# Message layer of a graph network kernel: five sums of halves moved between radial groups, and the rotation of older sums moved behind the new rotated features

## The reference

```python
x = _layernorm(x + _L0_gnn_ref(x, src, dst))        # mean of x[src] over the edges of each node
R = relu(edge_weight[:, None] @ w1 + b1) @ w2 + b2   # 64 hidden, 384 radial weights of each edge
# per edge: features x[src] = 8 scalars and 8 vectors; messages are sums over
# R * (spherical harmonics of the edge's direction) * features, by angular momentum
out = zeros.at[dst].add(msg)
x = _layernorm(x + out)
```

## Time and profile before

| | us |
|---|---|
| median of 3 runs | 4083.58 (4083.02 to 4086.64) |
| profiled execution, its own time | 4087.7 |
| its span | 4086.0 |
| PE busy | 3442.0 (84%) |
| DVE busy | 3366.2 (82%) |
| POOL busy | 2994.6 (73%) |
| ACT busy | 694.0 (17%) |
| message layer, from the first gather to the last batch | about 1830 to 3910 |

### The profile page before, as it was taken

One profiled execution on the slowest core, in us unless ns is written; L12 is line 12 of the kernel. 1 busy time (PEld: TensorE's weight loads), 2 busy tenths in 40 slices (PEclk: granted clock), 3 DMA queues, 4 the chain that ended last, 5 costly groups with the idle time before them and its releaser, 6 DMA issues.

```text
span 4086.0 us, 47708 instructions
## 1 busy us (share of the span) xinstructions
PE 3442.0 (84%) x14069; PEld 1822.3 (45%) x14069; DVE 3366.2 (82%) x4410; ACT 694.0 (17%) x1038; POOL 2994.6 (73%) x3050
## 2 busy tenths in 40 slices
PE   1988888888988888537999999999999999999963
PEld 0544444444444444333444444444444444444443
DVE  8877777767767776657999999999999999999965
ACT  0111111111111111101222212222222222122210
POOL 2777777777777777677777777777777777777747
PEclk9999999999999999658999999999999999999975
DMA  3111111111111111111222222222222222222211
GB/s 74 39 29 39 31 39 28 39 29 40 29 29 38 31 39 28 30 35 41 52 58 58 58 57 53 55 58 58 58 56 52 58 58 58 57 53 55 58 31 24
DMA packets 169732, 185.26 MB, mean 45 GB/s; under 512 B 57906, under 2 KB 136805, under 8 KB 163175
## 3 DMA queue, kind: packets, MB, share of 16 engines
q1 hardware_dynamic: 72486, 134.98, 11.8%
q0 software_dynamic: 97216, 49.97, 8.7%
HBM read 122.11 MB, written 62.61 MB: 45 GB/s over the span
## 4 chain that ended last, share of the span: by engine, by line
POOL 30%; issue 16%; PE 6%; DVE 2%; DMA 0%; POOLq 0%; DVEq 0%; ACT 0%
POOL got L559 27%; PE ps_r L822 3%; POOL hid L535 2%; PE ps_m L796 2%; PE ps_m L813 1%; DVE prod L1393 1%; DVE unit L1342 0%; DVE prod L1385 0%; DMA got<-x_d,idx 0%; DVE x_room L1342 0%; PE ps_m L805 0%; DVE part L1363 0%; POOLq L565 0%; POOLq L554 0%; DVE runs L1176 0%
## 5 line engine op out<-in xcount | busy, mean ns | idle before, releaser
L559 POOL DMA_INDIRECT got<-x_d,idx x1568 | 1575.2, 1005 | 510.3 <-issue 496.1
L822 PE MATMUL ps_r<-wc,hid 128*128 128x384 f32 x3136 | 1114.9, 494 | 136.8 <-DVE prod L1393 123.1
L822 PEld LDWEIGHTS ps_r<-wc,hid 128*128 128x128 f32 x3136 | 580.8, 190 | 677.4 <-DVE prod L1393 252.3
L1385 DVE TENSOR_TENSOR prod<-ps_r,f_along 128x768 f32<-128x768 f32 (+1 forms) x588 | 505.1, 859 | 105.3 <-PE ps_r L822 77.3
L750 PE MATMUL ps_r<-rest_f,hid 128*128 128x448 bf16 x1372 | 512.3, 373 | 0.2
L750 PE MATMUL ps_r<-inv_len,hid 128*128 128x448 bf16 x1372 | 510.1, 372 | 0.0
L750 PE MATMUL ps_r<-w_sb,hid 128*128 128x448 bf16 x1372 | 508.3, 370 | 0.0
L1393 DVE TENSOR_TENSOR prod<-ps_r,f_across 128x768 f32<-128x768 f32 (+1 forms) x588 | 505.6, 860 | 0.0
L512 POOL DMA_INDIRECT got<-in_x_dram,idx_deep x364 | 356.7, 980 | 184.0 <-issue 104.9
L512 POOL DMA_INDIRECT f_along<-in_x_dram,idx_deep x364 | 345.4, 949 | 111.0 <-issue 104.3
L512 POOL DMA_INDIRECT f_across<-in_x_dram,idx_deep x364 | 344.3, 946 | 111.0 <-issue 103.7
(11 more groups left out here) (189 smaller groups left out, 4199.5 us busy)
## 6 DMA issues: line engine op xcount, KB each, us to landing
run_d<-runs_t SPq DMA_DIRECT2D x196, 256.0 KB
hid<-weight_t SPq DMA_DIRECT2D x98, 512.0 KB, 5.8
got<-x_d,idx POOLq DMA_INDIRECT x1568
frame_d<-x_sb SPq DMA_DIRECT2D x7, 1008.0 KB, 4.4
frame<-frame_d SPq DMA_DIRECT2D x98, 72.0 KB
frame_b<-frame_d SPq DMA_DIRECT2D x98, 72.0 KB, 1.9
got<-in_x_dram,idx_deep POOLq DMA_INDIRECT x364, 2.4
f_along<-in_x_dram,idx_deep POOLq DMA_INDIRECT x364, 2.4
```

Source lines behind the costliest of these rows:

```text
L559: pool.indirect_dma_start(got[k][:, t, :], None, x1_d, bass.IndirectOffsetOnAxis(ap=idx[k][:, t:t + 1], axis=0)).then_inc(got2_landed[k], 16)
L822: mm = pe.matmul(ps_r[:, g % 2, t, 0:RD], hid[k][:, col:col + P], wc[:, :], start=True, stop=True)
L1385: dve.tensor_tensor(prod[q][:, 0:size, 0:2, :, :], ps_r[:, q, 0:size, 0:256].rearrange("p t (b v u) -> p t b v u", b=2, u=MUL), spread(f_a ...
```

## The change

On PE the sums of halves between the groups are (3), (4, 5) and (6, 7) in place of (3, 4), (5, 6) and (7). On DVE the rotation back of batch b - 2 comes behind the new rotated features in place of ahead of them.

```diff
                     radial(b, k, 2)
                     if not isinstance(b, int) or b > 0:
-                        add_halves(b - 1, 1 - k, (3, 4))
+                        add_halves(b - 1, 1 - k, (3,))
                     radial(b, k, 3)
                     if not isinstance(b, int) or b > 0:
-                        add_halves(b - 1, 1 - k, (5, 6))
+                        add_halves(b - 1, 1 - k, (4, 5))
                     radial(b, k, 4)
                     if not isinstance(b, int) or b > 0:
-                        add_halves(b - 1, 1 - k, (7,))
+                        add_halves(b - 1, 1 - k, (6, 7))
                     radial(b, k, 5)
...
                         halve(b - 1, 1 - k, GROUPS - 1)
-                    if not first:
-                        turn_back(b - 2, k)
                     s.settle()
                     s.mark(dve.tensor_tensor(part[:, 0], part[:, 0], part[:, 1], ALU.add))
                     s.settle()
...
                     dve.tensor_tensor(f_across[k][:, :, 0, :, :], part[:, 0, :, 1:3, :], part[:, 2, :, 1:3, :],
                                       ALU.add).then_inc(rotated_in, 1)
+                    if not first:
+                        turn_back(b - 2, k)
                     dve.wait_ge(f0_copied, b + 1)
                     dve.wait_ge(rotated_in, b + 1)
```

## The result

| | us |
|---|---|
| before, median of 4 runs | 4084.61 (4083.02 to 4086.64) |
| after, median of 4 runs | 4147.04 (4135.96 to 4173.83) |
| ratio | 1.0162, 95% interval 1.0140 to 1.0184 |
| predicted | 4184, range 4072 to 4245 |
| profiled run of after | 4173.83, span 4172.1 |

The change made the kernel 1.6% slower. The profiled run of after is the slowest of its four, so its trace shows somewhat more than the median pays. First the page of after: span, busy shares, the chain that ended last, and the group of the gathers.

What follows compares the result with a forecast made beforehand. Before, GpSimd and the VectorE/TensorE loop were taken as equally long; after, GpSimd bounds: 22.2 against 21.17 us over 97 batches, +100 us, 4188 for the profiled execution, 4184 as median, range 4072 to 4245.

Steps and rivals of the forecast that it cites:

- Steps 1 to 3: Message layer: regrouped halves and later rotation back bring the DVE and PE loop from 21.04 to 20.18 us.
- A3: DVE's first product of the fourth group, forecast 12.29 us after the batch's parts begin, before 13.14.
- GpSimd becomes the bound: Message layer: without holds GpSimd needs 20.30 us a batch, already more than the 20.18 of DVE and PE.
- The holds: Time gathers are held up by VectorE instructions with both inputs in SBUF; bounds 0.94 and 2.5 us a batch.
- by any phase: Mean hold if gathers start anywhere in the batch: 0.104 us a gather, 1.66 a batch.
- walked: Gather starts followed one by one from the parts: holds 2.1 us, then 2.0; 22.3 a batch with stops.
- The prediction's condition: A gather starting while VectorE runs an instruction with both inputs in SBUF is held until about 0.12 us before its end.
- the stops: GpSimd halts for about 2 us once in 112 gathers, 0.28 us a batch.
- step 1: PE: one half instead of two between radial 2 and radial 3, taking 0.86 us off the loop.
- A: Rival: GpSimd sheds its holds, 20.30 to 20.8 us a batch, 4000 to 4048 us; chance 0.14.
- B: Rival: the phase stays lucky or radial 3 gains nothing, 21.2 to 21.4 a batch, 4086 to 4106 us; chance 0.16.
- C: Rival: each batch collides with the hid load and holds reach 2.5, 22.8 a batch, 4242 us; chance 0.10.

Runs made afterwards that it cites:

- experiment 3: After, with SyncE's 512 KB load of hid queued behind the load of frame_b, nothing left out: 4104.3 us, 1.0047 of before.
- experiment 2: VectorE's part alone: before, with only the rotation back moved behind f_across, the halves as they were: 4162.2 us, 1.0179 of before.
- experiment 5: After, with two extra products of the third group, making VectorE's loop 0.94 us longer: 4154.9 us, 1.0177 of before.
- experiment 1: TensorE's part alone: before, with only the halves regrouped as 3, 4 to 5 and 6 to 7: 4097.6 us, 1.0027 of before.
- experiment 6: After, with each sum of halves replaced by a one-input copy of the first half, the second left out: 4122.5 us, 1.0099 of before.

## Why the prediction was right, and where it wasn't

The direction, the place and GpSimd as the bound came as forecast, the size was 37 us lower, 4147 in place of 4184, for the profiled execution 14 us. The traced execution took 4173.8 where the sum gave 4188 for it; what makes the other three runs 25 to 38 us shorter than that one, no trace shows, but their granted clock over the whole run is 0.925 to 0.926 against its 0.919, which fits fewer late landings.

- **Steps 1 to 3, the loop of DVE and PE.** Forecast A3 at 12.29, period 20.18; measured 12.11 and 20.18 in an undisturbed batch. Right.
- **GpSimd becomes the bound.** Right: 44 late landings for 127 us were measured where 40 or more for over 130 were named, and experiment 3 shows each batch beginning on GpSimd's last landing.
- **The holds.** Forecast 1.66 by any phase and 2.1 walked; measured 1.46. The walk's single holds are in the traces to 0.03 us (experiment 2). Why the mean of after is lower is mostly the 104 gathers that begin with an instruction and aren't held: held, they would bring it to 2.08 by the estimate above, near the walk's 2.1. The prediction's condition ("starts while VectorE runs" such an instruction) gave them no exception. That a late landing moves GpSimd to phases that cost less (a phase is where in DVE's batch the gathers begin) shows in VectorE's part alone and in experiment 5 (1.03 and 0.97 of holds in batches that waited, 1.94 and 1.80 in the others), hardly in after (1.38 and 1.51). L559's mean of 1036 ns is below the 1045 named.
- **Further idle.** Forecast 0.28 for the stops; measured 0.63, and this is the term that was missing. A late landing can cost more than the wait: in 24 of the 44 TensorE's clock falls behind it, the fourth product waits for up to 2.9, and GpSimd, then ahead, is stopped at its third gather for the radial groups (57 us against 12). For the same reason L1385's waits for PE were not nearly gone (53 us). The two misses had opposite signs: 1.46 + 0.63 = 2.09 against a chosen 22.2 - 20.0 = 2.2. That the sum came so near is in part luck.
- **The cause as the prediction divided it.** It let the shorter loop (step 1) bring the loss and took the rotation's place for harmless in itself. That step failed: the rotation's place alone costs 1.8%, TensorE's part alone 0.3%. The prediction had named the windows that the new order puts together, but not asked what they cost at the old loop. That a shorter loop raises the holds isn't refuted by this: with the free starts counted in, the old order would pay 0.33 more of them a batch in experiment 1, and it is these free starts that kept the holds there at 0.83.
- **Rivals.** A fell (the change brought more holds, not fewer), B fell (holds of 1.46 where it kept them near 1, and a fourth product that came earlier), C was partly there: 44 of 93 batches wait for a landing, not each.
- **The condition for a hold** was too narrow on one side (experiment 6), which changed nothing in the sum, since no one-input copy runs in this layer, and too wide on the other, at an instruction's beginning, which did.

Shown by runs: that the rotation's place carries the loss (experiment 2), that the load of hid beside a last landing costs 0.40 of idle (experiment 3), and that VectorE's work doesn't set the time (experiment 5). Read from traces and not tested by itself: what the free starts save, what the fall of the clock costs apart from the landing, and what a late landing does to the phase. The table's figures of holds and idle come from one profiled execution of each kernel. The run that would have shown GpSimd as the bound directly, after with 15 gathers, ran only where before itself was slow.

## What to carry to other kernels

Where an engine with a fixed step runs beside another that holds it up for the length of single instructions, the order of those instructions is a cost of its own: put instructions that don't hold (here those with a PSUM input) between those that do, and book the slower engine's time as steps, holds and idle before shortening the other loop. A gain in a loop whose partner is as long buys nothing but collisions; look at what lands beside what first. A large load that can be issued anywhere in a batch belongs away from the last small transfer that the next batch waits for: moved here, it gave back 43 of 62 us. Whether moving it would help the kernel before, where 6 landings came late, wasn't run.

## What the runs showed of the hardware, unexpected

- Data that land 1.5 us behind the gather's end (experiment 3) took 4.9 beside a 512 KB load issued 1.5 us ahead of that end; 3.4 was the figure of before.
- TensorE idle for 4.76 us came back at a granted 0.58, and needed 5.25 us for what takes 2.84; idle for 2.3 and 2.56 us it kept its full clock in the trace of before, idle for 2.47 it didn't in that of experiment 3 (4.46 us for the same six).
- A one-input copy of SBUF data (0.55 us for 128x768) holds a gather to 0.13 us ahead of its end, as a two-input sum does, and also prolongs by 0.09 to 0.16 us one that began some 0.4 us ahead of it, as no sum did.
- 104 gathers that began within 0.03 us of the beginning of a two-input instruction were not held in the trace of after; 61 others were.
- Undisturbed gathers step by 1.25 us in every kernel here. The same program took 4084 us in some sets and 4912 to 5156 in others (5156 and, ten minutes later, 4085 on the same chip), with TensorE's clock at 0.86 to 0.87 in its first 1800 us.
